# A narrower memset in front of every gather of the first of two graph layers

## The reference

```
h = relu(layernorm(x));  x = x + L0(h)      # score of an edge: leaky_relu(a_src[src] + a_dst[dst])
h = relu(layernorm(x));  x = x + L1(h)      # score of an edge: q[dst].k[src]/4 + edge_attr @ We + be
# in both: weights = softmax of the scores over the edges that share a target node,
# output of a node = sum of weight * value[src] over its edges
```

## Time and profile before

| | us |
|---|---|
| median of 3 runs | 1520.3 |
| lowest and highest of them | 1502.91 and 1521.98 |
| the profiled execution, its own time | 1507.14 |
| span of the profiled execution (first to last instruction) | 1505.4 |
| GpSimd busy in that span | 1213.3 (81%) |
| TensorE, VectorE, ScalarE busy | 954.2 (63%), 931.1 (62%), 635.1 (42%) |

### The profile page before, as it was taken

The page is one execution under the profiler, slowest core; times in us unless marked ns, Lnnn a source line. Parts: engine busy times, 40 slices in busy tenths (PEclk is TensorE's granted clock), DMA queues, the critical chain, the costliest instruction groups (busy, mean ns, idle before and its releaser), DMA issues.

```text
span 1505.4 us, 21963 instructions
## 1 busy us (share of the span) xinstructions
PE 954.2 (63%) x4985; PEld 801.6 (53%) x4985; DVE 931.1 (62%) x3002; ACT 635.1 (42%) x1699; POOL 1213.3 (81%) x1806
## 2 busy tenths in 40 slices
PE   5546575756657575755575667576666667676775
PEld 4335464545545454634454566465555556575654
DVE  6446565665656565656753666566666666666668
ACT  5624344343434343442168244434434444434404
POOL 5888888888888888886038888888888888888820
PEclk9656655666555666566597687777878777776765
DMA  6222222221222222222133333333333333333211
GB/s 140 70 68 47 68 47 67 47 68 47 67 47 69 47 66 47 62 46 82 49 107 88 87 89 88 88 88 88 89 88 90 88 88 88 88 88 88 86 31 43
DMA packets 54209, 110.41 MB, mean 73 GB/s; under 512 B 16876, under 2 KB 30848, under 8 KB 53956
## 3 DMA queue, kind: packets, MB, share of 16 engines
q0 software_dynamic: 36288, 91.12, 23.2%
q1 hardware_dynamic: 16483, 17.39, 4.2%
q10 hardware_dynamic: 1313, 0.50, 0.1%
HBM read 100.60 MB, written 8.81 MB: 73 GB/s over the span
## 4 chain that ended last, share of the span: by engine, by line
POOL 38%; issue 6%; DVE 5%; PE 3%; ACT 1%; DMA 0%; DVEq 0%; POOLq 0%; SPq 0%; ACTq 0%
POOL G L493 28%; POOL pad_i L479 10%; PE bank L826 2%; DVE halves L1048 1%; DVE acc L1402 1%; DVE mv L1055 0%; DVE G L1542 0%; DVE hn L1550 0%; DVE xs L1496 0%; DVE hn L1495 0%; DVE hn L1494 0%; PE bank L873 0%; ACT hn L547 0%; DVE G L1539 0%; DVE hn L1493 0%
## 5 line engine op out<-in xcount | busy, mean ns | idle before, releaser
L493 POOL DMA_INDIRECT G<-table,idx_all x880 | 869.0, 988 | 143.1 <-issue 120.2
L826 PE MATMUL bank<-PV,S 128*125 128x144 f32 x1760 | 435.4, 406 | 105.2 <-DVE PV L1379 83.6
L826 PEld LDWEIGHTS bank<-PV,S 128*125 128x125 f32 x1760 | 361.9, 279 | 134.1 <-issue 120.2
L1402 DVE TENSOR_TENSOR acc<-acc,bank 125x144 f32 x880 | 260.5, 296 | 175.7 <-PE bank L826 113.8
L479 POOL MEMSET pad_i<- 1x332 int32 x880 | 321.5, 365 | 17.6 <-DMA table<-h0b 8.8
L597 ACT ACTIVATE S<-iota_n,lid 128x125 f32<-128x125 f32 x880 | 275.7, 386 | 0.7 <-DVE pen L1143 0.7
L810 PE MATMUL bank<-qe,ST 125*128 x880 | 150.3, 325 | 57.7 <-DVE prod L1199 41.8
L810 PEld LDWEIGHTS bank<-qe,ST 125*128 125x128 f32 x880 | 132.4, 230 | 67.4 <-issue 66.5
L1379 DVE TENSOR_TENSOR PV<-G,PV 128x512 f32<-128x512 f32 x220 | 150.8, 686 | 18.9 <-issue 18.8
L601 ACT ACTIVATE S<-S,ones 128x500 f32<-128x500 f32 x220 | 156.6, 712 | 7.2
L607 ACT ACTIVATE ST<-bank 125x512 f32<-125x512 f32 x110 | 66.8, 607 | 218.8 <-PE bank L797 141.7
(11 more groups left out here) (220 smaller groups left out, 1241.7 us busy)
## 6 DMA issues: line engine op xcount, KB each, us to landing
G<-table,idx_all POOLq DMA_INDIRECT x880
prod<-in_edge_attr_dram SPq DMA_DIRECT2D x8, 672.0 KB
table<-G SPq DMA_DIRECT2D x12, 224.0 KB
bias_rows<-qe SPq DMA_DIRECT2D x1, 1664.0 KB, 5.8
table<-h0b SPq DMA_DIRECT2D x8, 178.5 KB
out_dram<-G SPq DMA_DIRECT2D x8, 168.0 KB
prod<-in_edge_attr_dram SPq DMA_DIRECT2D x8, 90.0 KB
xs<-in_x_dram SPq DMA_DIRECT2D x1, 504.0 KB
```

The lines of the kernel that those rows point to most:

```text
L493: pool.indirect_dma_start(G[:, u, v, 0:w], None, table, bass.IndirectOffsetOnAxis(ap=idx_all[:, g * GV + v:g * GV + v + 1], axis=0)).then_ ...
L826: last = pe.matmul(sums_bank(p)[0:BN, at:at + H * SLOT], S[:, ur, v, :], PV[:, v, :, :].rearrange("p h k -> p (h k)"), start=True, stop=True)
L1402: ve.tensor_tensor(a, a, o, ALU.add).then_inc(s.sem["acc_added"], 1)
```

## The change

In `gathers` the width of the memset depends on the layer `n`: 280 columns in layer 0, 332 in layer 1 as before. Nothing is added, removed or moved; both layers keep 440 memsets and 440 gathers in the same order with the same waits.

```diff
                         wait(pool, s["pv_ready"], 4 * (g - UNROLL) + j + 1)
                         for v in range(QV * j, QV * j + QV):
-                            space(332)
+                            space(332 if n else 280)
                             pool.indirect_dma_start(
                                 G[:, u, v, 0:w], None, table,
```

## The result

| | before | after |
|---|---|---|
| median, us | 1516.25 (4 runs on the chip of the comparison, 1502.91 to 1521.98) | 1538.38 (4 runs, 1536.05 to 1543.18) |
| profiled execution, span | 1507.14, 1505.4 | 1536.61, 1534.9 |
| ratio after / before | | 1.0166, interval 1.0112 to 1.022 |

The account below looks back on a forecast made before the run. GpSimd's beat of memset and gather was taken to bound the kernel. Layer 0's saving, 6.7 us dense to 20.4 us sparse, middle 13.5 us, gave 1520.3 - 13.5 = 1507 us, range 1483 to 1524.

Parts of the forecast that it names:

- GpSimd as pacemaker: Layer 0: GpSimd never waits for VectorE and sets the beat of memset, 0.16 us and gather, 1.476 us.
- The price of 52 columns: Layer 0's memsets: 0.83 ns per column, so 43 ns each and 19.1 us gross gain over 440 memsets.
- The holds: Layer 0 gathers starting during VectorE's two-input SBUF operations are held: 1.15 us a group if dense, 0.64 if sparse.
- Nothing else is late next: VectorE, TensorE and ScalarE keep some 6 us of slack a group, so GpSimd's saving in layer 0 reaches the end.
- The sum: Whole kernel: dense pattern saves 6.7 us, sparse 20.4 us, middle 13.5 us, giving 1507 us on the median's footing.
- the beat isn't the memset's: Gathers' queue or transfers may not accept one every 1.433 us for long; time stays at 1520; chance 0.12.
- The slower rival: Layer 0: VectorE's products hold more gathers, 25.7 us a group, 31 us slower, about 1551; chance 0.07.
- Layer 1 unchanged: Layer 1 keeps its width, its gathers begin after `table1` is written with phases set anew; change 0.

Follow-up runs that it names:

- e11: Kernel before with memsets of 306 columns instead of 332 in groups 0 to 21 of both layers, 332 in the last six; ratio 0.9925.
- e16: Kernel before with 306 columns in groups 0 to 21 of both layers, 332 in the last six, timed again on another chip; ratio 0.993.
- e7: Kernel before with the memset in bf16 and 350 columns instead of 332 in both layers; ratio 1.0091.
- e4: Kernel before with layer 0's memset at 280 columns and a second memset of 16 columns before each gather; ratio 1.0337.
- e6: Kernel before with ten more TensorE signals a group in layer 0, on a semaphore nobody waits for; ratio 1.0.
- e8: Kernel before, unchanged, profiled again on the chip of the run with bf16 memsets of 350 columns; 1505.31 us.
- e14: Kernel before with memsets of 280 columns in only the last six groups of layer 0, 332 elsewhere; ratio 1.0024.
- e3: Kernel before with layer 0 kept at 332 columns and layer 1 narrowed to 280; ratio 1.0412.

## Why the prediction was wrong

- **GpSimd as pacemaker: right before the change, not after it.** It set the beat, and waited for nobody. After, it waited 37.2 us for VectorE.
- **The price of 52 columns: right.** 43 ns predicted, 365 - 321 = 44 measured; unheld gathers stay at 0.95 us.
- **The holds: right in kind, too large.** The rule held: this product and this gather of the kernel after,

```profile
287.65 0.67 DVE L1379 TENSOR_TENSOR PV<-G,PV 128x512 f32<-128x512 f32 x1
287.71 1.45 POOL L493 DMA_INDIRECT G<-table,idx_all  x1 [0.16 <-POOL pad_i L479]
```

  give 287.71 + 1.45 - 0.95 = 288.21, against 0.12 us before the product's end, 288.20. But only 62 gathers of layer 0 were held, by 12.3 us in all (before: 94, 18.9), 0.4 us a group instead of 0.64 to 1.15. The offsets had been counted from `raw` as hung on the last gather, and that no longer was so.
- **"Nothing else is late next": the step that failed.** "VectorE keeps some 6 us of slack, and so do TensorE and ScalarE" was read correctly from the earlier trace rows, and taken as fixed. The slack is what is left after the chain from VectorE to TensorE and back, several times a group, and in more than half of the groups some of these returns got 1 to 7 us longer when the beat fell by 43 ns. Six us of slack don't cover two returns of 3.1 and 4.1 us, as on the timeline above. The trace of before had a sign of it in layer 1, among its waits from 780 to 1440 us:

```profile
ACT ST L607 <- remote: 19.3, 5, 4.3
DVE acc L1402 <- remote: 15.6, 7, 2.9
```

  At 1.476 us the slack still swallowed these.
- **The sum.** The forecast was 13.5 us less; the medians show 22.1 us more. In layer 0, GpSimd's memsets gave 440 x 0.044 = 19.4 us and its shorter holds 18.9 - 12.3 = 6.6; the waits for `pv_ready` took 37.2. That makes +11.2, and +11.7 was measured. The 17.4 us behind the layer had no term in the prediction at all.
- **The rival "the beat isn't the memset's"** had asked whether something accepts a gather every 1.433 us for long, and looked for the answer in the gathers. Its evidence, 0.95 us with no creep, held, and the gathers were indeed accepted at 1.43 us. The cost turned up on TensorE's signals, which are on none of the rows read. The price of this rival was also bounded at zero, without a reason that excluded a loss. The slower rival (products take the beat) did not happen.
- **Layer 1 unchanged: right** (+1.3 us), as is its phase set anew.

What makes TensorE's signals late is **not settled**. Shown: it comes with closely issued gathers, in both layers; it does not need their bytes or rows; it strikes signals from TensorE, while in the kernel after those between VectorE and ScalarE took 0.03 us as a rule and 0.35 at most, and those from VectorE to GpSimd 0.06; and its size differed between the runs on different chips, and between executions on one. That the gathers' own completions share a path with TensorE's signals would fit, but no run measured it.

## What to carry to other kernels

The slack of an engine that waits on the pacemaker is a reading at the present beat: before a pacemaker is made faster, list the round trips of signals inside the slack, and look in the trace for the first late ones (here lines 607 and 1402 in layer 1). A lag that builds up in a pipeline costs nothing while slots are free and time is left to work it off, and all of it at a barrier, so the place for a faster beat is the middle of a loop and not its last groups. A step of 2% and less on a shared resource should be timed on several chips: this one edit came out at 1.0166, 0.996 and 0.9981. Why the chips differ stays open.

## What the runs showed of the hardware that was not expected

- In layer 0 many of TensorE's completion signals reached VectorE and ScalarE 1 to 12 us late when gathers were issued every 1.38 to 1.45 us (e11 and e16, at 1.451 to 1.455 us, had few), and nearly all in 0.04 us at 1.49 us (e7) and 1.58 us (e4). At 1.473 to 1.477 us line 1309 was on time in the profile of before, in e6, in e8 and in the first 22 groups of e14, with line 645 late once or twice, and line 1309 was late 17 times in e3.
- Moving fewer rows did not help where it shortened the beat: 16 instead of 128 rows a gather, 0.86 instead of 0.95 us of GpSimd, beat 1.38 us, ratio 1.0377.
- On the chip of the first comparison 52 more columns of a memset that nobody reads, 19.4 us of GpSimd's time, made the kernel 22 us faster (1516.25 against 1538.38).
- A memset of 16 columns took 102 ns, of 105 columns 178, of 240 288, of 280 321, of 306 343 to 345, of 332 365.
